# Joined loop of a two-layer Perceiver block: the heads' variance spread by one product, its root on ScalarE, its inverse on VectorE

## What is computed

```python
o = gla_scan(q * dk ** -0.5, k, v, gk) + sigmoid(aug_w[..., None] * v)
mu = o.mean(-1, keepdims=True)            # over the 32 values of a head
var = o.var(-1, keepdims=True)
o = (o - mu) * rsqrt(var + 1e-5)
x = x + silu(g) * o @ Wout
n = layernorm(x)                          # (x - mean) / sqrt(var + 1e-5), over 512
x = x + dequant(quant(n)) @ dequant(quant(weight)).T + bias
n4 = layernorm(x)                         # the rows for the next cross attention
```

## Time and profile before

| | |
|---|---|
| median of 3 runs | 1162.43 us (1161.41 to 1163.83) |
| the profiled execution, its own time | 1162.92 us |
| its span, first to last instruction | 1161.7 us |
| TensorE busy | 1134.4 us, 98% |
| VectorE busy | 749.6 us, 65% |
| ScalarE busy | 537.0 us, 46% |
| GpSimd busy | 245.0 us, 21% |
| mean granted TensorE clock | 0.998 of full |

### The profile page before, as it was taken

The page is one execution under the profiler, slowest core; times in us unless marked ns, Lnnn a source line. Parts: engine busy times, 40 slices in busy tenths (PEclk is TensorE's granted clock), DMA queues, the critical chain, the costliest instruction groups (busy, mean ns, idle before and its releaser), DMA issues.

```text
span 1161.7 us, 21747 instructions
## 1 busy us (share of the span) xinstructions
PE 1134.4 (98%) x8729; PEld 845.6 (73%) x8729; DVE 749.6 (65%) x1523; ACT 537.0 (46%) x1036; POOL 245.0 (21%) x308
## 2 busy tenths in 40 slices
PE   7999999999999999999999999999999999999997
PEld 4655488775658777777777777777888678887886
DVE  6367488769794656666566666665797866546632
ACT  3244456653122655655565656565554532223421
POOL 2300013256640342121212222211432100000000
PEclk9999999999999999999999999999999999999999
DMA  9759710100305265444444444454710502224211
GB/s 348 278 216 397 284 40 1 60 23 1 109 19 182 36 137 101 91 92 93 91 92 92 92 91 100 92 102 77 109 18 1 82 2 35 37 37 76 34 37 36
DMA packets 325671, 111.57 MB, mean 96 GB/s; under 512 B 301834, under 2 KB 302908, under 8 KB 321348
## 3 DMA queue, kind: packets, MB, share of 16 engines
q1 hardware_dynamic: 324224, 109.11, 37.3%
q10 hardware_dynamic: 1348, 1.09, 0.4%
HBM read 65.59 MB, written 20.97 MB: 75 GB/s over the span
## 4 chain that ended last, share of the span: by engine, by line
PE 88%; DVE 7%; SPq 2%; issue 1%; ACT 1%; DMA 1%; POOL 0%; DVEq 0%; ACTq 0%
PE bank L303 66%; PE bank L1961 3%; PE bank L583 2%; PE bank L601 2%; PE bank L1977 2%; PE bank L259 2%; SPq L1860 2%; PE bank L1163 1%; PE bank L519 1%; DVE stats L227 1%; DVE Am L1379 1%; PE bank L2434 1%; PE bank L1185 1%; PE bank L1130 1%; DMA W<-in_L_xattn_kernel_k_dram 1%
## 5 line engine op out<-in xcount | busy, mean ns | idle before, releaser
L1898 POOL COPY PT<-W 32x512 f32<-32x512 f32 x120 | 84.0, 700 | 308.4 <-DVE W L2111 210.8
L2100 DVE CUSTOM_DVE_ANT_0 W<-bank,W 128x512 f32<-128x512 f32 x128 | 80.8, 687 | 102.0 <-PE bank L1961 98.5
L2191 ACT ACTIVATE K<-bank,vecT 128x512 f32<-128x512 f32 x64 | 43.8, 690 | 164.4 <-PE bank L303 164.4
L2212 ACT ACTIVATE W<-W,low 128x512 f32<-128x512 f32 x128 | 90.7, 711 | 16.9 <-DVE low L2100 16.9
L303 PE MATMUL bank<-xT,wT 128*128 128x512 f32 x384 | 92.6, 390 | 0.8 <-ACT W L3150 0.5
L303 PE MATMUL bank<-Wkv,Wq 128*128 128x512 f32 x384 | 92.7, 395 | 0.0
L303 PE MATMUL bank<-Wkv,ctxT 128*128 128x512 f32 x384 | 92.0, 395 | 0.0
L303 PE MATMUL bank<-ctxT,Wkv 128*128 128x512 f32 x384 | 90.0, 392 | 1.2 <-DVE ctxT L320 1.2
L303 PE MATMUL bank<-Wq,Wkv 128*128 128x512 f32 x384 | 89.7, 389 | 0.0
L303 PE MATMUL bank<-woT,hR 128*128 128x512 f32 x384 | 87.8, 390 | 0.7 <-DVE W_late L3062 0.5
L303 PEld LDWEIGHTS bank<-Wkv,ctxT 128*128 128x128 f32 x384 | 70.8, 188 | 22.1 <-ACT K L2191 5.7
(11 more groups left out here) (377 smaller groups left out, 2119.0 us busy)
## 6 DMA issues: line engine op xcount, KB each, us to landing
PT<-W SPq DMA_DIRECT2D x360, 64.0 KB, 2.1
W<-ctx_turned SPq DMA_DIRECT2D x16, 1024.0 KB, 5.7
W<-in_ctx_dram SPq DMA_DIRECT2D x8, 1024.0 KB, 10.6
ctx_turned<-ctxT SPq DMA_DIRECT2D x8, 1024.0 KB, 7.7
ctx_turned<-W SPq DMA_DIRECT2D x8, 1024.0 KB, 6.7
XT<-in_ctx_dram SPq DMA_DIRECT2D x4, 1024.0 KB, 11.8
XT<-in_L_ffn_wi_dram SPq DMA_DIRECT2D x64, 64.0 KB, 2.1
raw_own<-in_ctx_dram SPq DMA_DIRECT2D x3, 1024.0 KB, 11.3
```

The lines of the kernel that those rows point to most:

```text
L1898: pool.tensor_copy(there, here).then_inc(kept_p.s, 1)
L2100: dve.tensor_tensor_reduce(out=PR[:, j, :], in0=bank[:, 4 + j % 4, :], in1=mask, scale=1.0, scalar=3.0e38, op0=ALU.add, op1=ALU.min, accum ...
L2191: act.activation(K[:, m, :], bank[:, n % 4, :], ACT.Identity, bias=pcol("L1_xattn_bk", m)).then_inc(ring_a.s, 1)
L2212: act.activation(PR[:, j, :], PR[:, j, :], ACT.Exp, bias=low[:, j:j + 1], scale=-1.0, accum_out=total[:, j:j + 1]).then_inc(expd.s, 1)
```

## The change

The variance now comes out in the same layout as `y`: one product of the whole matrix `block` (1/32 within a head's 32 features, 0 elsewhere) with the squares gives 128 x 512 variances, each repeated over its head. ScalarE takes the root of variance plus epsilon (`Sqrt`, with a bias tile `eps`), VectorE takes the reciprocal over 128 x 512 and then multiplies `y` by it. `variance_v`, `deviation_pool`, `widen_a` and `widen_pe` are gone. For groups 0 and 1 the variance is first copied out and the root taken later (`early_root_a`), after ScalarE's last sigmoid.

The rows' layer norm ahead of the quantisation moves from VectorE to ScalarE (`normalise_rows_a`): `rstd * X + shift`, for which VectorE makes minus the mean (`negated`) and GpSimd multiplies it by `rstd`.

In the order of the engines: `normal_v` of group `t-2` now stands after step `t`'s masks (it was group `t-3`, ahead of them), `key_weights_v` in steps 2, 3, 6 and 7 instead of 2 to 5, ScalarE's sigmoids in steps 1 and 2. On TensorE a quarter of the gate's or the projection's products is put ahead of `mean_of_pe`, and the wait for `sg_v(2)` stands after the scores.

```diff
-            if l == 1 and g >= G // 2 or l == 5:
+            if l == 1 and g >= G // 2 or l in (2, 5):
                 p(ins)
                 ins = pool.tensor_tensor(shift[:, g:g + 1], shift[:, g:g + 1], rstd[:, g:g + 1], ALU.mult)
...
             def variance_pe(g):
                 pe.wait_ge(sqr.s, sqr(g))
-                for t in range(C):
-                    ins = pe.matmul(bank[:, 5, 4 * t:4 * t + 4], sq_at(g)[:, t * P:(t + 1) * P], block[:, 0:P:GDV], start=True, stop=True)
-                ins.then_inc(var_pe.s, 1)
-
-            def widen_pe(g):
...
+                pe.matmul(bank[:, 5, :], block[:], sq_at(g), start=True, stop=True).then_inc(var_pe.s, 1)
...
-                    if 3 <= t < G + 3:
-                        widen_pe(t - 3)
...
+                    if 3 <= t < 6:
+                        project_pe(t - 3, range(1))
                     if 1 <= t < 6:
                         mean_of_pe(t - 1)
...
             def normal_v(g):
-                dve.wait_ge(wide_pe.s, wide_pe(g))
+                if g < 2:
+                    dve.wait_ge(root_a.s, root_a(g))
+                else:
+                    dve.wait_ge(var_a.s, var_a(g))
                 dve.wait_ge(gated.s, gated(g))
-                dve.tensor_tensor(y[:, g % 3, :], y[:, g % 3, :], bank[:, 6, :], ALU.mult).then_inc(ynm.s, 1)
+                v(dve.reciprocal(root_at(g), root_at(g)))
+                dve.tensor_tensor(y[:, g % 3, :], y[:, g % 3, :], root_at(g), ALU.mult).then_inc(ynm.s, 1)
...
             def stats_of_v(l, g):
                 dve.wait_ge(xsum.s, summed(l, g))
-                row_stats_v(g)
+                row_stats_v(g, negated=l == 1)
 
             def quantise_v(g):
                 rows = xq[:, g:g + 1, :]
-                normalise(xq, 2, g)
-                dve.wait_ge(normed.s, normed(nth("normed", 2, g)))
+                dve.wait_ge(normed_a.s, normed_a(G // 2 + g))
...
-                    if 3 <= t:
-                        normal_v(t - 3)
                     for r in range(4):
                         masked_v(t, r)
+                    if 3 <= t:
+                        normal_v(t - 2)
...
+                    if t == 2:
+                        dve.wait_ge(proj.s, proj(GATE + 7))
+                        key_weights_v(0)
                     if t < 3:
                         gate_last_v(5 + t)
-                    if 2 <= t <= C + 1:
-                        key_weights_v(t - 2)
-                    if 1 <= t:
-                        variance_v(t - 1)
+                    if t == 2:
+                        normal_v(0)
+                    if t in (3, 6, 7):
+                        key_weights_v({3: 1, 6: 2, 7: 3}[t])
...
                 for g in (5, 6, 7):
                     add_v(g)
-                    if g < 7:
-                        normal_v(g + 1)
+                    if g == 5:
+                        normal_v(7)
...
+            def variance_a(g):
+                act.wait_ge(var_pe.s, var_pe(g))
+                if g < 2:
+                    act.copy(root_at(g), bank[:, 5, :]).then_inc(var_a.s, 1)
+                else:
+                    act.wait_ge(ynm.s, ynm(g - 1))
+                    act.activation(root_at(g), bank[:, 5, :], ACT.Sqrt, bias=eps[:]).then_inc(var_a.s, 1)
+
+            def early_root_a(g):
+                act.wait_ge(var_a.s, var_a(g))
+                act.activation(root_at(g), root_at(g), ACT.Sqrt, bias=eps[:]).then_inc(root_a.s, 1)
+
+            def normalise_rows_a(g):
+                act.wait_ge(rstd_ok.s, rstd_ok(nth("rstd", 2, g)))
+                act.activation(xq[:, g, :], X[:, g, :], ACT.Identity, scale=rstd[:, g:g + 1],
+                               bias=shift[:, g:g + 1]).then_inc(normed_a.s, 1)
```

More of the change, by code:

```diff
@@ L1029, in gpsimd @@
                     row_stats_pool(1, g)
-                p(pool.memset(half[:], -0.5))
+                p(pool.memset(eps[:], EPS))
                 p(pool.memset(augw[:], 0.0))
@@ L1143, in variance_pe, with project_pe @@
                 pe.wait_ge(sqr.s, sqr(g))
-                for t in range(C):
-                    ins = pe.matmul(bank[:, 5, 4 * t:4 * t + 4], sq_at(g)[:, t * P:(t + 1) * P], block[:, 0:P:GDV], start=True, stop=True)
-                ins.then_inc(var_pe.s, 1)
-            def widen_pe(g):
[L1149 to L1164, removed]
+                pe.matmul(bank[:, 5, :], block[:], sq_at(g), start=True, stop=True).then_inc(var_pe.s, 1)
+            def project_pe(g, chunks=range(C)):
+                if 0 in chunks:
+                    pe.wait_ge(ynm.s, ynm(g))
+                    if g:
+                        pe.wait_ge(xsum.s, summed(2, g - 3) if g in (3, 4) else summed(1, g - 1))
+                for c in chunks:
+                    ins = pe.matmul(bank[:, 7, :], y[:, g % 3, c * P:(c + 1) * P], slot(7)[:, c, :], start=(c == 0),
+                                    stop=(c == C - 1), skip_group_check=True)
+                if C - 1 in chunks:
+                    ins.then_inc(proj.s, 1)
             def turn_blocks_pe(g):
                 pe.wait_ge(scaled.s, scaled(g))
-                if g + 2 < G:
-                    pe.wait_ge(ynm.s, ynm(g + 2))
                 if g:
@@ L1249, in value_pe, with gate_pe @@
                 ins.then_inc(proj.s, 1)
-            def gate_pe(u):
+            def gate_pe(u, chunks=range(C)):
                 m, n = u % C, u // C
@@ L1254, in gate_pe @@
                     pe.wait_ge(low_w.s, low_w(C - 1))
[L1255 to L1260, removed]
+                if 0 in chunks:
+                    if u < 4:
+                        pe.wait_ge(taken_a.s, taken_a(QK[1] - G + u))
+                    else:
+                        pe.wait_ge(sg_a.s, sg_a(u - 4))
+                ins = product(bank[:, 4 + u % 4, :], lambda h, k: Wmix[:, h, chunks[k], m * P:(m + 1) * P],
+                              lambda h, k: xb(h, chunks[k], n * 512, 512), len(chunks), first=0 in chunks, last=C - 1 in chunks)
+                if C - 1 in chunks:
+                    ins.then_inc(proj.s, 1)
             def aug_sums_pe():
@@ L1323, in tensor @@
                     if t in (1, 2):
-                        gate_pe(5 + t)
+                        gate_pe(5 + t, range(1, C))
                     if 6 <= t:
@@ L1331, in tensor @@
                     if 3 <= t:
-                        project_pe(t - 3)
+                        project_pe(t - 3, range(1, C) if t < 6 else range(C))
                     if 1 <= t <= G:
@@ L1546, in vector @@
                 low_of_v(7)
-                normal_v(5)
+                normal_v(6)
                 quantise_v(4)
-                variance_v(7)
                 for g in (5, 6, 7):
                     add_v(g)
-                    if g < 7:
-                        normal_v(g + 1)
+                    if g == 5:
+                        normal_v(7)
                     stats_of_v(1, g)
@@ L1753, in scalar @@
                         gate_out_a(5 + t)
+                    if t == 1:
+                        for g in (3, 4, 5):
+                            sigmoid_a(g)
+                    elif t == 2:
+                        early_root_a(0)
+                    if 4 <= t < G + 4:
+                        normalise_rows_a(t - 4)
                     if t >= 5:
                         blocks_a(t - 5)
-                    if t <= C:
-                        key_weights_a(t - 1)
+                    if 3 <= t <= 5:
+                        key_weights_a(t - 2)
+                    if t <= G:
+                        variance_a(t - 1)
+                    if t == 2:
+                        early_root_a(1)
+                        key_weights_a(0)
                     if t == G + 3:
```

63 lines of the change are left out of this document (24 added, 39 removed).

## The result

The changed kernel takes **1186.76 us** (median of 4 runs, 1186.08 to 1187.40); the kernel before, in the same session, 1162.44 (1161.41 to 1163.83). The ratio is 1.0204, 95% interval 1.0192 to 1.0217: 24.3 us slower, where the prediction's sum was 17.1 slower (1180.0, range 1170 to 1188).

The account below looks back on a forecast made before the run. VectorE was taken to bound steps 4 and 5 and the tail, and steps 6 to 8 once it exceeds TensorE's need. 6.7 + 6.8 + 3.6 = 17.1 us on 1162.92 gave 1180.0 us, range 1170 to 1188.

Parts of the forecast that it names:

- own range of the forecast: Whole kernel: 1177 to 1187 us, from 3 us under the forecast time to 7 over if GpSimd slows more of VectorE.
- clock rival: TensorE's idle gaps bring slow products; cost in half of step 3, last linear product, next part's keys: 1186 us, 12%.
- if the granted clock is below 1.00 there: Sign that the prediction is wrong: TensorE's granted clock falls below 1.00 in steps 4 to 7.
- TensorE's busy time: Whole change: four transposes fewer in each group, variance product added, about 3 us less work, costed at nothing beside late VectorE.
- The price of the reciprocal: VectorE, 128x512, once in each of eight groups: 3.35 us, from the line through the short sizes.
- Steps 0 to 3: Loop's start: weight differences and early reciprocals delay step 4 from 263.12 to 269.8, +6.7 us.
- Steps 4 and 5: Middle of the loop: VectorE's listed work makes each step 11.2 us long.
- Steps 6 and 7: End of the loop: VectorE's work gives 14.9 and 15.4 us, TensorE needs about 12 and sets nothing.
- The tail, to the end of the last quantisation: After the loop: 28.1 us of VectorE's work plus waits makes 32.6 us, +3.6 us.
- Nothing after the tail gives time back: Next part: it starts with VectorE's splits and then TensorE's full stretch, so none of the loss is recovered.
- The wide reciprocal is cheap: Rival for all eight groups: short sizes mislead, reciprocal below about 1.3 us, kernel about 5 us faster, 1158 us, 10%.
- Idle hides more: Rival: VectorE's idle halves the first steps' +6.7 us and the tail's new waits vanish, about 1173 us, 10%.

Follow-up runs that it names:

- e1: The changed kernel with its eight wide reciprocals replaced by a multiplication by 1.0 of the same tile: 1167.09 us, ratio 1.0031.
- e2: The changed kernel with the wide reciprocal done twice in each group: 1213.28 us, ratio 1.0428.
- e5: The changed kernel with step 2's weight differences (`key_weights_v(0)`) moved into step 3, behind the normals: 1184.60 us, ratio 1.0184.
- e7: The changed kernel with ScalarE's root replaced by its inverse root (`Abs_reciprocal_sqrt`) and VectorE's wide reciprocal removed: 1164.80 us, ratio 1.0012.
- e8: The kernel of e7 with the two orders of e3 and e5 added: 1160.57 us, ratio 0.9978 to the kernel before.
- e3: The changed kernel with `linear_v` put ahead of `normal_v`, which holds the reciprocal, in steps 6 and 7: 1183.12 us, ratio 1.0162.
- e4: The changed kernel with unused products added in TensorE's gaps, seven in step 3, four and three in steps 6 and 7: 1181.83 us, ratio 1.0155.
- e10: The kernel before with only one wide VectorE reciprocal on `y` added per group in `normal_v`: 1191.35 us, ratio 1.0235.
- e6: The changed kernel with the rows' norm ahead of the quantisation back on VectorE: 1186.01 us, ratio 1.0197.
- e9: The kernel of e8 with the rows' norm of each group back on VectorE: 1161.23 us, ratio 0.9974 to the kernel before.

## Why the prediction was right, and where it fell short

The time lies within the range, 1.2 us from its upper end, and even within the own range of the forecast (1177 to 1187). That is in part luck. The upper end stood there for GpSimd slowing VectorE and for a clock rival that costs elsewhere, and by one of its own signs the prediction is wrong: it named "if the granted clock is below 1.00 there", in steps 4 to 7, and measured are 0.84, 0.95, 0.75 and 0.87 by stretch from 276 to 322. TensorE's busy time, forecast 3 us less, is 6.1 more. The 1180.0 was also counted from the profiled execution (1162.92); from the median the same sum gives 1179.5.

*The price of the reciprocal* was right: 3.34 us against 3.35, by the slope of the earlier trace rows. The estimate from the Trainium skill's page "VectorE: DVE Perf Modes", section "First, the fixed hardware budget" (repeat count 8, an estimated 4.4 us), is not borne out. Its time, 1188, would have lain nearer to the result than mine, for a reason that is not in it. The rate of 8.3 us of time for each us of reciprocal, which the prediction worked out, was somewhat high: e1 and e2 give 6.9 and 7.8.

*Steps 0 to 3*: +6.9 against +6.7, and for the reasons given: the weight differences stood in front of the last gate, 2.3 us of it (e5; 3.1 without the reciprocals, e7 against e8), and the rest is the two early reciprocals.

*Steps 4 and 5*: 11.18 and 11.19 against 11.2.

*Steps 6 and 7*: this is the step that failed. The prediction had 14.9 and 15.4 with "so it sets nothing there any more" about TensorE; measured were 17.7 and 16.8, **4.2 us more**. It counted what TensorE's products take at the full clock, 12 us, and not when they may start: group 3's projection needs the bank that `linear_v(0)` frees, and that now stands behind a reciprocal. e3 (order) and e4 (clock) each restore the two steps to 14.9 and 15.1, and 15.3 in both. The order alone would be covered; the gap that it makes, with the lower clock behind it, is not.

*The tail, to the end of the last quantisation*: 33.0 us against 32.6 (359.88 - 326.86). The waits for ScalarE's rows came as 2.00 and 1.17 where 2.1 and 1.1 had been worked out. The short waits of 0.4 and 0.9 at its start did not come. Instead the product with `y` at 330.84 took 1.77 us where it takes 0.69 elsewhere, while GpSimd multiplied by the gate (1.27 us from 330.80). So the tail's sum is close in part because two errors cancel.

*"Nothing after the tail gives time back"* held, but something is lost there: the offset grows from 21.9 us at the last quantisation to 23.3 at the end of the span. In the experiments on the changed chain it also grows, by 0.4 (e2) to 3.0 us (e5), and in e10, on the old chain, by 0.2. With the rows' norm back on VectorE it grows less (e6 0.9, e9 0.6 where e8 has 1.7). In the change 0.55 us of it shows as a wait of TensorE for a late row of VectorE in the next part, at 441.06; no run here was made to settle its cause. **1.4 us left open.** Another 1.0 is the difference between spans and medians.

Together: 0.2 + 4.2 + 0.4 + 1.4 + 1.0 = 7.2 us, the gap between 17.1 and 24.3.

*The rivals.* "The clock falls" was named with 12% and 1186, and the time came out by it, but not where it put it. It wanted the cost in half of step 3, in the last linear product and in the next part's keys; e4 shows that step 3 pays nothing. The cost came in steps 6 and 7, which it did not name. The Trainium skill's rule in "TensorE: Matmul & The Clock Gate", section "HAM oscillation — how this bites in real kernels", is that idle gaps between bursts bring the array back to its lower clock. The trace agrees with the direction: a granted clock of 0.74 to 0.87 in four of the five stretches above, which hold waits of 1.5 to 6.7 us or, for the one from 300, begin at the end of a wait of 4.34. "The wide reciprocal is cheap" would not even have given a gain: e1 and e7 stay above the kernel before, since steps 0 to 3 lose time to the order of the weights' differences (e7's step 4 begins 3.6 us later than before), and its 1158 had counted a gain of 5 us from the shorter chain. In e7, whose first steps still have that order, the rest of the change costs 0.12% in all; in e8, without it and with `linear_v` ahead, it gains 0.22%. "Idle hides more" failed: steps 0 to 3 lost 6.9 us and not half of it, the tail's waits came, and with the doubled reciprocal each microsecond cost 7.8 over eight groups.

## What to carry to other kernels

Price an operation that is new in size from the slope of the sizes that the trace does show, and look for the same function on the engine that already touches the tile: root and reciprocal in one ScalarE function of 0.69 us made a 24 us loss into a wash, and with two changes of order into a small gain. When a long instruction is put into an engine's list, go through what stands behind it for whatever frees a bank or buffer for another engine, and move that ahead. If TensorE then idles and restarts slowly in a place where another engine waits for it, the cost is larger than the gap; the same slow restart costs nothing where TensorE has slack.

## What the runs showed of the hardware

- VectorE's reciprocal grows close to linearly from 1 column to 512, by 6.0 ns a column up to 16 and 6.2 from there: 163 ns at 1, 253 at 16, 3341 at 512, in float32 at 128 partitions. A scale by 1.0 of the same tile took 0.43 us in the median (e1).
- ScalarE's `Abs_reciprocal_sqrt` took 0.69 to 0.72 us for 128x512, as its root did. The table load ahead of it took 1.28 us (250.75 in e7), directly behind one instruction and directly ahead of the next.
- A projection whose eight records take 3.60 to 3.67 us took 5.37 behind a wait of 2.86 us, and 6.28 behind one of 4.34 in the change but 5.37 behind one of 4.34 in e5. The length of the wait alone does not settle the size. Unused products in the wait made it 3.60 (e4).
